# Residual rows made ahead, routing work spread over steps, and value products issued before the last fills of a step, in a two-layer transformer kernel

## The reference

```python
def _L0_attn_ref(x, rms_w, wq, bq, wk, bk, wv, bv, wo, bo):
    residual = x
    xn = rms_norm(x, rms_w)
    ...
    scores = jnp.where(causal, scores, -jnp.inf)
    probs = jax.nn.softmax(scores, axis=-1)
    out = jnp.einsum('bhst,bthd->bshd', probs, v).reshape(B, S, KEY_DIM)
    return out @ wo + bo + residual
...
probs = jax.nn.softmax(xr @ Wg, axis=-1)
gate_vals, expert_idx = jax.lax.top_k(probs, K)
pos = jnp.sum((jnp.cumsum(oh, axis=0) - 1) * oh, axis=1)   # place of a token in its expert
dispatched = xr[dispatch_mask.reshape(-1) % S].reshape(E, C, d)
```

## Time and profile before

| what | value |
|---|---|
| median of 3 runs | 1108.1 us (1107.91 to 1111.09) |
| profiled execution, device time | 1110.99 us |
| its span, first to last instruction | 1109.3 us |
| mean granted TensorE clock | 0.922 of full |
| PE, DVE, ACT, POOL busy | 87%, 54%, 43%, 38% of the span |

### The profile page before, as it was taken

How to read it: one execution, slowest core, us unless ns; L and a number is a source line. 1 busy time by engine, 2 the same in 40 slices (tenths; PEclk the granted TensorE clock), 3 DMA queues, 4 the chain that set the end, 5 groups by cost and what they waited for, 6 DMA issues and landing times. The chain is left out here.

```text
span 1109.3 us, 17911 instructions
## 1 busy us (share of the span) xinstructions
PE 960.0 (87%) x6142; PEld 766.7 (69%) x6142; DVE 601.8 (54%) x1986; ACT 477.1 (43%) x855; POOL 425.9 (38%) x402
## 2 busy tenths in 40 slices
PE   3799999987729999999973789799999769999996
PEld 1467666754419999999971546576667458888885
DVE  7577686866333434333335775766666324553544
ACT  2255555643204334333336254556556433343331
POOL 3352434324531333322246523445243534634232
PEclk9799999998658999999995888999999979999998
DMA  4442222210113332333113842523410010000001
GB/s 138 171 158 101 86 68 86 68 34 29 58 71 124 124 118 102 112 123 123 61 46 95 251 149 82 181 82 114 139 58 29 1 49 1 1 20 1 20 1 38
DMA packets 50313, 91.80 MB, mean 83 GB/s; under 512 B 7360, under 2 KB 23104, under 8 KB 50112
## 3 DMA queue, kind: packets, MB, share of 16 engines
q1 hardware_dynamic: 47168, 82.49, 22.1%
q0 software_dynamic: 3072, 8.39, 2.4%
HBM read 54.55 MB, written 36.31 MB: 82 GB/s over the span
## 5 line engine op out<-in xcount | busy, mean ns | idle before, releaser
L816 ACT ACTIVATE a_probs<-a_ps_b 128x512 f32<-128x512 f32 x320 | 187.3, 602 | 175.4 <-PE a_ps_b L882 173.4
L1100 DVE CUSTOM_DVE_ANT_0 a_masked_s<-a_ps_a,a_mask_f 128x512 f32<-128x512 f32 (+1 forms) x256 | 154.3, 621 | 113.7 <-PE a_ps_a L866 103.4
L866 PE MATMUL a_ps_a<-a_k_st,a_q_st 128*128 128x256 f32 (+3 forms) x512 | 191.2, 421 | 14.8 <-DMA a_k_st<-scratch 12.4
L520 POOL TENSOR_SCALAR_AFFINE_SELECT a_probs<-a_probs 128x512 f32<-128x512 f32 x128 | 80.1, 640 | 211.6 <-ACT a_probs L816 211.3
L1739 POOL TENSOR_TENSOR w_lo<-w_raw,w_hi 128x2048 fp32r<-128x2048 f32 x16 | 74.1, 4628 | 170.1 <-ACT w_hi L1756 170.1
L882 PE MATMUL a_ps_b<-a_q_less,a_k_st 128*128 128x384 f32 (+3 forms) x512 | 134.7, 327 | 5.0 <-ACT a_probs L816 4.1
L866 PEld LDWEIGHTS a_ps_a<-a_k_st,a_q_st 128*128 128x128 f32 x512 | 96.4, 200 | 55.2 <-issue 33.2
L882 PEld LDWEIGHTS a_ps_b<-a_q_less,a_k_st 128*128 128x128 f32 x512 | 90.2, 194 | 27.5 <-ACT a_probs L816 19.9
L906 PE MATMUL a_ps_pv<-a_probs,a_v 128*32 128x512 f32 (+3 forms) x1024 | 93.8, 491 | 1.1 <-POOL a_probs L520 1.1
L1804 DVE SCALAR_TENSOR_TENSOR exp_h_lo<-exp_ps_u,exp_h_hi 128x320 fp32r<-128x320 f32 x128 | 61.4, 490 | 58.9 <-ACT exp_h_hi L1765 58.1
L1765 ACT ACTIVATE exp_h_hi<-exp_ps_u 128x320 fp32r<-128x320 f32 x128 | 54.2, 439 | 89.5 <-PE exp_ps_u L1832 89.5
(11 more groups left out here) (278 smaller groups left out, 2201.7 us busy)
## 6 DMA issues: line engine op xcount, KB each, us to landing
w_raw<-in_m_w SPq DMA_DIRECT2D x16, 1024.0 KB, 5.6
scratch<-a_hi SPq DMA_DIRECT2D x24, 512.0 KB, 2.8
scratch<-a_lo SPq DMA_DIRECT2D x24, 256.0 KB, 3.1
a_q_st<-scratch SPq DMA_DIRECT2D x64, 96.0 KB, 2.7
a_k_st<-scratch SPq DMA_DIRECT2D x64, 96.0 KB, 2.7
exp_rows<-dispatched SPq DMA_DIRECT2D x9, 640.0 KB, 3.9
dispatched<-kept_sub SPq DMA_DIRECT2D x9, 512.0 KB, 2.9
results<-exp_out SPq DMA_DIRECT2D x7, 640.0 KB, 3.1
```

Source lines behind the costliest of these rows:

```text
L520: nc.gpsimd.affine_select(out=blocks, in_=blocks, compare_op=ALU.is_ge, fill=0.0, base=0, pattern=[[0, HPG], [1, P]], channel_multiplier=- ...
L816: nc.scalar.activation(probs[:, k, :], ps_b[k % B_BANKS][:, :], ACT.Exp, scale=scale).then_inc(exps, 1)
L866: last = nc.tensor.matmul(ps[:, at:at + wd], q_st[t % STACKS][:, h // PER_TILE, i * P:wd], k_st[t % STACKS][:, h, 0:wd], start=True, stop= ...
L1100: nc.vector.tensor_tensor_reduce(masked_s[n % 2][:, 0:wd], ps[:, 0:wd], mask_f[:, SEQ - wd:SEQ], -1.0, -NEG, ALU.add, ALU.min, nmax[:, t % ...
```

## The change

1. Layer 0: ScalarE writes `x * rstd` into a new buffer `resid` (`scaled`, 16 instructions of 128x256, in slots 1, 3, 6, 8 of steps 0, 4, 8, 12), GpSimd adds the output bias to it (`residual`, 8 instructions of 128x512, slots 5 and 10), and VectorE empties an `out` bank with one addition of 128x512. TensorE's 16 bias products and the tables behind them are gone.
2. Layer 0: the third sequence's `ot`, `out` and the routing entries are placed anew; `lg` is filled in four parts; the joins and routing steps of VectorE, and the scatters of GpSimd, move with them.
3. Both layers: `values_of_old` issues `pv` part 0 of the step before last in slot 1, then `max_unit` 2 (before in slot 2), then parts 1 and 3, all ahead of that slot's fills. A wait on `masked` now stands before part 0 (one select) and before part 1 (three selects).
4. Layer 1: `late` entries are emptied in slot 0 instead of slot 1.

```diff
-HALVED = ("pr", "v", "out", "lg")
+PARTS = {"pr": 2, "v": 2, "out": 2, "lg": TPB}
...
     def late(name, T):
-        put(name, T, 10, T + 1, 1)
+        put(name, T, 10, T + 1, 1 if rope else 0)
...
-        if rope and b == BATCH - 2:
-            put(("ot", b, 0), T + 2, 2, T + 2, 4)
-            put(("ot", b, 1), T + 2, 3, T + 2, 5)
-            put(("out", b, 0), T + 2, 5, T + 2, 7)
-            put(("out", b, 1), T + 2, 7, T + 2, 9)
...
+        early(("ot", b, 0), T + 2)
+        middle(("ot", b, 1), T + 2)
+        late(("out", b, 0), T + 2)
+        early(("out", b, 1), T + 3)
...
-        put(("rk", 0, 0), 14, 0, 14, 2)
-        put(("rk", 1, 0), 15, 0, 15, 2)
...
+        put(("ot", 2, 0), 14, 4, 14, 6)
+        put(("rk", 0, 0), 14, 9, 15, 0)
+        put(("rk", 1, 0), 15, 6, 15, 8)
...
+        put(("lg", 2, 0), 16, 9, 17, 2)
+        put(("rk", 2, 0), 17, 6, 17, 8)
...
+            def residual(b, half):
+
+                pool.wait_ge(scaled_rows, b * TPB + 2 * half + 2)
+                rows = resid[b % 2][:, 2 * half:2 * half + 2, :]
+                nc.gpsimd.tensor_tensor(rows, rows, bias_o[:, :].unsqueeze(1).to_broadcast([P, 2, D]),
+                                        ALU.add).then_inc(resid_ready, 1)
...
+            def scaled(b, i):
+
+                n = b * TPB + i
+                if b > 1:
+                    emptied(act, ("out", b - 2, i // 2))
+                nc.scalar.activation(resid[b % 2][:, i, :], tile(x, n), ACT.Identity,
+                                     scale=rstd[:, n:n + 1]).then_inc(scaled_rows, 1)
...
-                    if biased:
-                        pe.wait_ge(bias_split, 2)
-                        nc.tensor.matmul(ps[:, half * D:(half + 1) * D], spread_row[0:2 * VW, :], bias_rows[:, :], start=True,
-                                         stop=False)
...
+            def values_of_old(t):
+
+                if t % GROUPS == 0:
+                    emptied(pe, ("v", t // GROUPS, 0))
+                    emptied(pe, ("v", t // GROUPS, 1))
+                pe.wait_ge(masked, t * 4 + 1)
+                need(pe, pv_copied, t)
+                pv(t, 0).then_inc(pv_done, 1)
+                if t + 2 < STEPS:
+                    max_unit(t + 2, 2)
+                pe.wait_ge(masked, t * 4 + 3)
+                pv(t, 1)
+                pv(t, 3).then_inc(pv_done, 1)
...
-                        max_unit(T, s)
+                        if s != 2:
+                            max_unit(T, s)
                     if prob_at(T, s):
                         prob_unit(*prob_at(T, s))
+                    if s == 1:
+                        if 0 <= T - 2 < STEPS:
+                            values_of_old(T - 2)
+                        elif T < STEPS:
+                            max_unit(T, 2)
                     for name, half in FILLS_AT.get((T, s), ()):
                         fill(name, half)
-                    if s == 2 and 0 <= T - 2 < STEPS:
...
-                for i in range(2):
-                    last = nc.vector.scalar_tensor_tensor(tile(sub, n + i), tile(x, n + i), rstd[:, n + i:n + i + 1],
-                                                          bank(name)[:, i * D:(i + 1) * D], ALU.mult, ALU.add)
-                last.then_inc(free(name), 1)
+                dve.wait_ge(resid_ready, 2 * b + half + 1)
+                nc.vector.tensor_tensor(sub[:, n:n + 2, :], bank(name)[:, :].rearrange("p (i d) -> p i d", i=2),
+                                        resid[b % 2][:, 2 * half:2 * half + 2, :], ALU.add).then_inc(free(name), 1)
...
-            for n in range(6, 11):
+            for n in range(4, 10):
                     scatter(n)
                 root(0, BATCH - 1)
+                scatter(10)
+                root(1, BATCH - 1)
                 scatter(11)
```

104 lines of the change are left out of this document (40 added, 64 removed).

## The result

The changed kernel took 1101.8 us (median of 14 runs, 1093.9 to 1107.0), the kernel before 1114.2 beside it (14 runs); the ratio is 0.989 [0.9865, 0.9916]. That is 12 us faster where 31 were forecast, outside the range of 1064 to 1099: direction right, size wrong by more than half. A part of the absolute figure is its base: the forecast started from 1108.1 us (3 runs), and over the 14 runs the kernel before itself stands at 1114.2. One execution, the profiled one of e8, was in a slower state than the others and is left out of e8's ratio.

The account below looks back on a forecast made before the run. The prediction took TensorE, busy 87% of the span, as the bound. Its terms, -13.5 - 6.5 + 0 - 6.0 - 3.5 - 1.9 = -31.4 us against 1111.0, gave 1079.6, stated as 1079; range 1064 to 1099.

Parts of the forecast that it names:

- Layer 0 to step 13: Layer 0 before step 14: ended waits -1.8, new copy wait +5.7, bias products gone -3.9; sum 0, bounds -5 and +6.
- The wait for `a_q_less`: Layer 0: first probability product after the fill waits 0.48 us for ScalarE's copy, 11 times, plus 0.4 in step 1: 5.7.
- The bias products: Layer 0: each costs TensorE 0.49 us, eight lie in the full steps, so removing them gives -3.9 us.
- Layer 1: Layer 1: value products ahead of the fills remove 13.5 of 15.9 us of waits; the restored clock gives -6.5.
- the first rival: Waits move: VectorE falls behind in layer 1 and score products wait for banks; 1093 us in total, chance 17 in 100.
- The 0.34: Layer 1 clock term: loss per us at low clock, from value products taking 2.94 us instead of 1.93.
- a rest of 0.9 us: Layer 1: what stays where a step has two waits (3.1 us) against 2.2 us of work put ahead of the fill.
- Steps 14 and 15: End of layer 0: step 14 falls to 14 us, VectorE-bound step 15 gains 3.9; sum -6.0, bounds -9 and +1.
- Steps 16 and 17 and the tail: End of layer 0: -3.5 from fuller clock less the rank product's wait, and -1.9 mainly from four fewer bias products.
- The claim that the scatters behind the loop end before the root: Tail of layer 0: GpSimd's six scatters, formerly five, end before its root, as TensorE's `out` parts take longer.
- Short waits: Rival: the new 0.48 us wait in every layer 0 step lowers the clock; +13 us, 1092, chance 8 in 100.
- Slower by late selects: Rival: GpSimd's late selects stop the value products, now ahead of the fill, and all behind; about 1118, chance 9 in 100.

Follow-up runs that it names:

- e8: Changed kernel with GpSimd's root of the third output's variance behind the two selects of step 16, not ahead; ratio 0.980 to the kernel before.
- e7: Changed kernel with the score product of slot 2 ahead of all three value parts, making them one group; ratio 0.986 to the kernel before.
- e1: Changed kernel with the value products back behind the fills in both layers; ratio 0.981 to the kernel before.
- e4: Kernel before with only the residual buffer in place of the 8 bias products; ratio 0.994 to the kernel before.
- e5: Kernel before with one number changed: layer 1 banks filled in slot 10 are emptied in slot 0, not 1; ratio 0.989 to the kernel before.
- e13: The changed kernel, unaltered, run again beside its variants; 1091.0 us against 1112.9 for the kernel before, ratio 0.982.
- e9: Changed kernel with value products ahead in layer 1 only and GpSimd's root behind the selects of step 16; ratio 0.970 to the kernel before.
- e11: e9 with the third sequence's rank product and placing behind the last transposes, not ahead; ratio 0.970 to the kernel before.
- e16: e9 with e11's rank product behind the last transposes and e7's one group in layer 1; 1072.8 us, ratio 0.966 to the kernel before.
- e12: Changed kernel with the last of the three value parts behind the fills in both layers; ratio 0.983 to the kernel before.
- e6: Kernel before with the spread third output and routing slots alone; ratio 0.996 to the kernel before.
- e17: e16 with two of GpSimd's six scatters between the two roots and scatter 10 behind the second; ratio 0.974 to the kernel before.

## Why the prediction was wrong, step by step

**Layer 0 to step 13, forecast 0 from -1.8 + 5.7 - 3.9, measured +6.3: this step failed, by a term that it put at nothing.** The wait for `a_q_less` was foreseen to 0.05 us (0.53 for 0.48, 11 times, and part of a twelfth; the sum takes the copy's end as 129.35 where its row gives 129.30). What the sum left out is that splitting the value products adds two crossings to each step: 24 of them cost 3.2 us (e7). TensorE's other added work, 158.45 to 159.69, is 1.2 more (e1 against e7); what it is stays open, and at equal clock it is larger, as e1 has some 3 us at the low one. The idle time of the weight loads around the group could be read before, in a view that the prediction does not show:

```profile
128.84 0.16 PEld L906 LDWEIGHTS a_ps_pv<-a_probs,a_v 128*32 128x32 f32 x8 [0.35 <-issue]
130.70 0.19 PEld L866 LDWEIGHTS a_ps_a<-a_k_st,a_q_st 128*128 128x128 f32 x1 [0.20 <-issue]
```

I took the group as one total and did not ask how often its two ends are paid. The bias products gave 3.2 us of work, not 3.9, and in e4 only 1.2 of time, since VectorE's `a_nm` is close behind. The 1.8 us of waits for `a_nm` did end, and 1.1 for `a_nmax` came. In sum -3.2 + 3.2 + 1.2 - 1.8 + 5.8 + 1.1 = +6.3.

**Layer 1, forecast -13.5 - 6.5 = -20.0, measured -16.3.** TensorE's time without work in the stretch fell from 22.1 to 10.5 us, -11.6, and its busy time from 211.9 to 207.2, -4.6. The waits of the earlier trace rows vanished as forecast, all 15.9 us; 4.6 for `a_nmax` and one select (1.6) came, which is the first rival, at about a third of its price (3.7 of 10 us). The -4.6 is the clock and the same forgotten term together. The clock gave more than forecast, 0.41 to 0.50 us for each us less at the low clock, not 0.34, so some 9 us for 19.0; and 29 more crossings took some 4 back. The 0.34 was read from the value products alone, and the rest of TensorE's work loses more. The Trainium skill (TensorE: Matmul & The Clock Gate, HAM oscillation) puts the loss at half of the throttled time, and these traces bear that out better than the row that I let decide. The cause was also told too narrowly. I named the earlier emptying of the `late` banks as a help for a rest of 0.9 us; e5 shows that this one number is worth 10.4 us by itself (5.9 of waits, 4.5 of busy time by the clock), so most of the gain did not need the value products to move.

**Steps 14 and 15, forecast -6.0, measured -7.1.** Right in sum, and by the fills step 14 takes 14.4 us (forecast 14) and step 15 17.9 (forecast about 18). Step 15's figure is luck. I added 3.9 us because VectorE would have that much more to do, but e8, with the same work on VectorE, does the step in 14.6 us (250.52 to 265.13). What made it 17.9 is a cost that I placed in a rival: a select late by 3.9 us, not because selects follow ScalarE late but because a root waiting for VectorE stood ahead of them on GpSimd (e8: -4.0 us without it). VectorE is a limit there only at the end: in e8 the fill waits 1.64 us for `a_nm`.

**Steps 16 and 17 and the tail, forecast -5.4, measured +7.6 or, in e13, -3.8.** With TensorE's results on time the forecast is 1.6 us off; half of the time at the low clock is gone there (20.5 us before, 10.1 in e13), and the rank product waits 2.7 us (forecast about 2). In the first comparison the results were late, which no term of the prediction holds, and with 13.0 us this is the largest piece of the miss in that trace. That the late results are no property of this program alone is shown (e13); that they explain the whole difference of the ratios 0.989 and 0.982 is argued: 11.4 us of the 18.8 between the two profiled spans lie in this stretch, the rest in stretches that nothing in the program tells apart. The claim that the scatters behind the loop end before the root held in the changed kernel, in both of its traces, and fails once the tail is shorter (e9 and e11, where the root starts without idle time ahead of it, 0.8 and 3.5 us after the variance).

**Rivals.** Moved waits came in part. Short waits did not lower the clock: it is 1.00 from 60 to 250 us with a wait of 0.53 in each of 11 steps. Slower by late selects: one select in each layer, not every step.

## What to carry over

Count crossings between small and full matrix products, not only products: where TensorE has no idle time, cutting a group in two is paid in every step. Move work ahead of a wait only in the stage that has the wait; here the same edit was good for layer 1 and cost layer 0 7.1 us (e1 against the changed kernel) where the forecast had 3.9. And before a large reordering, try the smallest edit alone: one slot number brought two thirds of layer 1's gain.

## What the runs showed of the hardware

- A crossing between 32-column value products and 128-column products costs TensorE 0.12 to 0.15 us on average at full clock (layer 0: 24 crossings 3.2 us, another 24 3.5 us; layer 1: 28 crossings 4.0 us from e16 to e9, 29 more 3.4 us from e9 to e12), with no wait shown.
- A us at the low clock costs this kernel's mixed products 0.41 to 0.50 us of busy time (before and e5: 211.9 and 207.4 us busy with 23.9 and 12.9 us at the low clock, in the same order). Value products alone lost 0.34.
- Results of TensorE can be taken up late while nothing else waits, up to 4.9 us after the modelled end (e6, 292.4 us), near 280 to 300 us, at the start of layer 1 and near 700 us, while indirect DMAs run. All ten traces of the changed kernel, e1 to e8 and e17 have between one and eight such places; the kernel before and e9 to e16 have none. Copy to copy of `a_o_t` is then 1.5 to 2.8 us, where it is 0.85 in e13 at the same, low, granted clock (0.5 from 288.0 us on). Chip, program and clock do not separate these cases: one chip gave both (e6 and e13), and so did one program (the changed kernel and e13). The profiles do: in the same ten no landing of a scatter could be told, in the other nine it is 2.4 us after the issue. The scatters' own transfers end 2.1 us after the issue in the changed kernel and in e13 alike, so the transfers themselves are not slower. The cause stays open.
- Ratios of one kernel from different comparisons differed by more than their intervals (0.989 and 0.982), so small differences are only read within one comparison.
